# Attention on Trainium2: two query chunks side by side in the product for the maximum

## The reference

```python
h = _layernorm(x, axis=-1) * (1 + ca) + sa           # x: 16 x 512 x 256, float32
q = (h @ Wq.T).reshape(b, t, 8, 64)
kv_latent = h @ Wkv_down.T                           # 64 wide
k = (kv_latent @ Wk_up.T).reshape(b, t, 8, 64)
v = (kv_latent @ Wv_up.T).reshape(b, t, 8, 64)
scores = einsum('bqhd,bkhd->bhqk', q, k) * 64 ** -0.5
attn = softmax(scores, axis=-1)
out = einsum('bhqk,bkhd->bqhd', attn, v).reshape(b, t, 512)
x = x + ga * (out @ Wo.T)
```

## Time and profile before

| | |
|---|---|
| median of 3 runs | 1625.9 us (1625.34 to 1626.49) |
| the profiled execution | 1625.48 us, span of its instructions 1623.7 us |
| mean granted TensorE clock | 0.883 of 2.4 GHz |
| TensorE busy | 1327.1 us, 82% |
| VectorE busy | 1145.3 us, 71% |
| ScalarE busy | 740.7 us, 46% |
| GpSimd busy | 556.0 us, 34% |

### The profile page before, as it was taken

The page is one execution under the profiler, slowest core; times in us unless marked ns, Lnnn a source line. Parts: engine busy times, 40 slices in busy tenths (PEclk is TensorE's granted clock), DMA queues, the critical chain, the costliest instruction groups (busy, mean ns, idle before and its releaser), DMA issues. The chain is left out here.

```text
span 1623.7 us, 24084 instructions
## 1 busy us (share of the span) xinstructions
PE 1327.1 (82%) x5919; PEld 937.7 (58%) x5920; DVE 1145.3 (71%) x2512; ACT 740.7 (46%) x1442; POOL 556.0 (34%) x928
## 2 busy tenths in 40 slices
PE   6499999999999999999999999999511595979200
PEld 3266666666666666666666666666411595868200
DVE  2368877778777787777877778777367744656387
ACT  1366656556565565655656556564200003333052
POOL 1101423234232342323423234223310356667247
PEclk7599999999999999999999999999855556989655
DMA  4000011010110101101011010110120103232464
GB/s 108 14 14 27 1 53 49 4 52 0 53 48 4 53 0 52 47 6 52 0 53 50 3 40 1 40 40 1 44 54 0 52 0 82 36 85 33 116 220 142
DMA packets 68360, 70.29 MB, mean 43 GB/s; under 512 B 13568, under 2 KB 64176, under 8 KB 68160
## 3 DMA queue, kind: packets, MB, share of 16 engines
q1 hardware_dynamic: 44272, 44.82, 9.2%
q10 hardware_dynamic: 18960, 18.88, 3.5%
q0 software_dynamic: 5056, 5.85, 2.3%
HBM read 40.35 MB, written 28.92 MB: 43 GB/s over the span
## 5 line engine op out<-in xcount | busy, mean ns | idle before, releaser
L830 PE MATMUL PS<-PF,V 128*128 128x512 f32 x1024 | 523.9, 593 | 0.0
L561 ACT ACTIVATE PF<-PS 128x512 f32<-128x512 f32 x512 | 303.0, 595 | 345.0 <-PE PS L756 343.4
L733 DVE TENSOR_REDUCE NMAX<-PS 128x1 f32<-128x512 f32 x512 | 346.5, 687 | 160.7 <-PE PS L765 150.5
L755 PE MATMUL PS<-Q,K 128*128 128x512 f32 x512 | 405.8, 792 | 0.9 <-ACT PF L561 0.9
L531 POOL TENSOR_TENSOR XL<-XF,XH 128x512 fp32r<-128x512 f32 x64 | 84.2, 1316 | 445.7 <-ACT XH L636 445.7
L765 PE MATMUL PS<-K,Q 128*128 128x512 f32 x512 | 203.6, 398 | 6.0 <-DVE NMAX L733 5.9
L756 PE MATMUL PS<-Q,K 128*128 128x512 f32 x512 | 202.7, 396 | 0.0
L830 PEld LDWEIGHTS PS<-PF,V 128*128 128x128 f32 x1024 | 174.5, 189 | 36.2 <-issue 6.7
L579 ACT ACTIVATE Q<-PS 64x512 fp32r<-64x512 f32 x256 | 151.5, 592 | 67.8 <-PE PS L93 63.0
L755 PEld LDWEIGHTS PS<-Q,K 128*128 128x128 f32 x512 | 97.2, 190 | 123.5 <-issue 105.4
L756 PEld LDWEIGHTS PS<-Q,K 128*128 128x128 f32 x512 | 97.4, 190 | 121.7 <-issue 121.6
(11 more groups left out here) (286 smaller groups left out, 2534.6 us busy)
## 6 DMA issues: line engine op xcount, KB each, us to landing
X<-in_L_attn_x SPq DMA_DIRECT2D x16, 512.0 KB, 5.0
MODB<-mod_rows SPq DMA_DIRECT2D x16, 512.0 KB, 4.4
h_rows<-H ACTq DMA_DIRECT2D x16, 512.0 KB, 3.1
acc_rows<-H ACTq DMA_DIRECT2D x16, 512.0 KB, 4.1
A<-acc_rows SPq DMA_DIRECT2D x16, 512.0 KB, 8.3
out_x<-X SPq DMA_DIRECT2D x16, 512.0 KB, 2.9
W1F<-in_L_ffn_W SPq DMA_DIRECT2D x3, 1024.0 KB, 4.9
W2F<-in_L_ffn_W SPq DMA_DIRECT2D x3, 1024.0 KB, 5.8
```

The lines of the kernel that those rows point to most:

```text
L561: s_exp.done(act.activation(PF[:, u % 4, :], st_bank(u), ACT.Exp))
L733: s_mred.done(dve.tensor_reduce(NMAX[:, h % 2, c:c + 1], mx_bank(u), AX.X, ALU.max, negate=True))
L755: pe.matmul(st_bank(u), K1[:, kp, keys], Q1[:, h, :], start=True, stop=False)
L830: s_pv.done(pe.matmul(pv_bank(h), V1[:, vp, c, :], PF[:, u % 4, :], start=(c == 0), stop=(c == TC - 1)))
```

## The change

The contraction of the product for the maximum is cut to 64 rows: high part times high part. A second copy of the latent's high part, K3, stands in rows 64 to 127, so that a chunk can be multiplied on either half of the array. The units are taken in pairs in the even slots: the even unit uses rows 0 to 63 (Q1, K1), the odd one rows 64 to 127 (Q1, K3), and both are issued one behind the other. The pair waits for the reduce of unit u-1 in place of u-2. ScalarE makes K3 with one more copy for each batch, VectorE's L720 waits for that copy too, and the semaphore counts of the latent's copies move.

```diff
-                    ("K2", [P, 2, T], F32R), ("Q2", [P, H, T], F32R),
+                    ("K2", [P, 2, T], F32R), ("K3", [P, 2, T], F32R), ("Q2", [P, H, T], F32R),
...
-    s_exp, s_qhi, s_latc, s_v, s_nf = S("exp", UNITS), S("qhi", 16), S("latc", 3), S("vv", 1), S("nf", KC)
+    s_exp, s_qhi, s_latc, s_v, s_nf = S("exp", UNITS), S("qhi", 16), S("latc", 4), S("vv", 1), S("nf", KC)
...
                             s_latc.done(act.activation(K1[0:R, jp, :], bank[0:R, :], ACT.Copy))
                             s_vt.wait(act, jb - 1, 0)
                             s_latc.done(act.activation(LTF[:, :], bank, ACT.Copy))
+                            s_latc.done(act.activation(K3[R:P, jp, :], bank[R:P, :], ACT.Copy))
                             s_latc.wait(act, jb, 0)
                             s_latc.done(act.activation(K2[0:R, jp, :], K1[0:R, jp, :].bitcast(F32), ACT.Copy))
...
                         elif kind == "lat":
-                            s_latc.wait(dve, jb, 1)
+                            s_latc.wait(dve, jb, 2)
...
                     tb, u = unit(b, n + AHEAD)
-                    if exists(tb):
+                    if exists(tb) and u % 2 == 0:
+
                         h, c, kp = u // TC, u % TC, (par + (n + AHEAD) // UNITS) % 2
-                        s_mred.wait(pe, tb, u - 2)
+                        s_mred.wait(pe, tb, u - 1)
                         if c == 0:
                             s_qlo.wait(pe, tb, h)
+                            s_latc.wait(pe, tb, 3)
                             s_klo.wait(pe, tb, 0)
-                        s_mx.done(pe.matmul(mx_bank(u), Q1[:, h, c * P:(c + 1) * P], K1[:, kp, :], start=True, stop=True))
+                        s_mx.done(pe.matmul(mx_bank(u), Q1[0:R, h, c * P:(c + 1) * P], K1[0:R, kp, :], start=True, stop=True))
+                        s_mx.done(pe.matmul(mx_bank(u + 1), Q1[R:P, h, (c + 1) * P:(c + 2) * P], K3[R:P, kp, :], start=True, stop=True))
...
                         elif kind == "vt":
-                            s_latc.wait(pe, jb, 2)
+                            s_latc.wait(pe, jb, 1)
```

More of the change, by code:

```diff
@@ L329, in attention @@
     MODB = sb("MODB", [P, 4, D])
-    K1, K2 = sb("K1", [P, 2, T], F32R), m["K2"]
+    K1, K2, K3 = sb("K1", [P, 2, T], F32R), m["K2"], m["K3"]
     V1 = m["V1"]
```

## The result

The changed kernel takes 1694.7 us (median of 4 runs, 1694.2 to 1694.9) against 1625.6 before (median of 4; the three runs of the table above gave 1625.9): ratio 1.0428, 95% interval 1.041 to 1.0446. It is slower by 69 us, inside the range (1650 to 1738) and in the forecast's own range, 15 us under its point of 1710.

The account below looks back on a forecast made before the run. TensorE was taken to bound attention. Pairs at 4.3 us a batch plus waits at 1.0 made 5.3, over 16 batches +85 us on 1625.5: about 1710 us, own range 1690 to 1735, 8-in-10 range 1650 to 1738.

Parts of the forecast that it names:

- The bound: Attention, two thirds of the execution: TensorE is its bound, busy 1062.6 of 1068.0 us.
- The change of shape: TensorE at each pair: a 0.10 us drain each way and loads laid bare; pair +0.27 us, 4.3 a batch.
- B: Rival: no drain, overlap works, VectorE decides; about 1653 us, or 1605 if only two stretches bind; chance 0.12.
- C: Rival: neither drain nor overlap, only the waits are new, +3.4 us a batch, about 1680 us; chance 0.10.
- D: Rival: drains cost nothing, VectorE draws ahead so reduces are not late; 1566 us at full price; chance 0.07.
- the two rows: Set-up profile rows, 16 to 128 columns and 128 to 64 rows: each next load comes 0.10 us late.
- The second load, +0.11: Within a pair on TensorE: the upper half's load follows the lower half's, 0.11 us; if hidden, pair +0.16.
- What would show it: Signs in the profile after: late loads, spacing of product records, waits in slots 16 and 4, a 73.0 us batch.
- the one for the hidden load: Sign at a pair: the two product records start under 0.01 us apart if the second load is hidden.
- The late reduce: Pairs on TensorE wait for VectorE's reduce of u-1 instead of u-2: +1.0 us a batch above the pairs.
- A: Rival: drains, but the two products don't overlap; +0.39 us a pair, about 1734 us; chance 0.13.
- The K3 copy at nothing: ScalarE's extra copy, 0.62 us, is hidden by 2.3 us before L720; uncovered, 0.6 a batch, 9 us.

Follow-up runs that it names:

- the doubled pair: Changed kernel with both reduces in the even slot, each pair issued twice in a row: 1720.3 us, 55.6 above the same kernel with pairs issued once.
- the four corners: Pairs on full or 64 rows, odd reduce late or beside the even one: full 1676.6 and 1626.6 us, 64 rows 1694.7 and 1664.7 us.
- The run on one half: Changed kernel, but the second product of a pair also uses rows 0 to 63 (Q1, K1): 1734.7 us, ratio 1.067.
- full rows: Changed kernel's order, waits and K3 copy, but both products of a pair use all 128 rows: 1676.6 us, ratio 1.0314.

## Why the prediction was right, and where it was off

**The bound.** Right. TensorE was full, and what was laid on it in attention came out in the time: one more pitch a pair, in the doubled pair, came back as 55.6 us of the 60 that 256 pitches make. A batch takes 71.8 us, not 73.0.

**The change of shape.** Right in mechanism, place and size of its parts. The load of the first product starts 0.33 us after its predecessor, as given; the drain on the way back, which was my choice without a row, is the same 0.10 (0.43 from load to load is 0.11 load, 0.23 stream, 0.10 drain), and it holds for fp32r as for the float32 of set-up. Rivals B, C and D, which have no drain, fell with that. One of the two rows it was read from is weaker than I took it for. It was a step from 16 to 128 columns of weights, but in attention before the change the transpose of the maxima has 4 columns between neighbours of 128, and no drain shows on either side: each load starts with the product that was issued before it (L765 has its record at 853.39, L776 at 853.62).

```profile
853.39 0.08 PEld L776 LDWEIGHTS PS<-IDENT,NMAX 128*4 128x4 f32 x1
853.62 0.30 PEld L830 LDWEIGHTS PS<-PF,V 128*128 128x128 f32 x2 [0.15 <-issue]
```

What made the load of 18.43 late in set-up is open. The row on 128 and 64 rows, the change that the kernel makes, is the one that the runs bear out.

**The second load, +0.11: the term that was mis-sized.** I let the load for the upper half follow that for the lower one. They start together, within 0.01 us, and the pair costs +0.16 by the rows, 0.149 by the four corners (0.14 by their traces), not +0.27. 16 x 0.11 x 16 = 28 us too much. This was named as the lower end (+0.16), and of the signs under "What would show it" the one for the hidden load came true. The run on one half shows what the estimate described: a load 0.11 behind the first when both go to the same rows. With +0.16 a pair the prediction's own terms come to 2.56 + 0.92 + 0.46 + 0.1 - 0.1 = 3.9 us a batch, or about 1689 us, the lower end of its own range (1690). The 1694 that it gives for a hidden load doesn't come out of these terms, and that 1694.7 was measured is no support for it. The Trainium skill, TensorE: Matmul & The Clock Gate, section Measured speedup vs the span model, has tiles start about 4 ns apart, and the trace agrees for the products: 3 ns in the median of 256 pairs.

**The late reduce.** Right in mechanism, and larger than in the sum: a second term that was mis-sized. Slots 14 to 16: +1.08 predicted, +1.09 measured. Slots 0 to 4: +0.78 predicted and 0.78 measured. Slots 20 to 22 and 26 to 28: I gave 0.1 above the pairs for both together, and it is 0.73 - 0.16 = 0.57 and 0.26 - 0.16 = 0.10. That is 9 us too little. I had assumed that the dearer pairs would cover these delays, and for slots 20 to 22 that was wrong whatever a pair costs: the stretch is 0.73 longer here, 0.63 with full rows and 0.74 with both products on one half, where a pair costs 0.39. Like the chain of slots 14 to 16 it hangs on the product of its own first slot: after that come its reduce, the statistics, the low part of the queries (two L702) and the reduce of slot 21 (for the wait ahead of the pair of slot 22 the profile names L702 at most of the loads and the reduce at most of the products). Rival B's reading for it, +0.6, was nearer. Since the pairs are cheaper, slots 0 to 4 and 14 to 16 stand out by 0.46 and 0.93 above them and not by 0.24 and 0.81, 5 us more. The wait of slot 19 that vanished, -0.36 a batch or 6 us, I hadn't seen. Of the signs, TensorE waits in slot 16 for 0.9 us and not 0.8, in slot 4 for 0.4 and not 0.2, in slots 6 and 10 for nothing, and it also waits in slot 22, which I hadn't named.

So in attention the forecast is 28 us too high for the second load, 6 too high for the wait that went, and 14 too low for late reduces: 20 too high, and the traces have 65 us where it had 85. That the point is off by 15 us only is in part luck: the misses have different signs, and the 4 us behind attention, which the change doesn't explain, make the rest.

**The rivals.** A (no overlap), 1734: the kernel built like that takes 1734.7. That it fits to 1 us is luck as well: A lacked the +0.35 of slots 20 to 22 and the -0.36 of the wait that vanished, and the two cancel. C (only the wait), 1680: the kernel built like that takes 1676.6. The terms of B add up to +1.8 a batch and not to +1.7, which is 2 us. B and D need an array that changes shape for nothing; there is no such kernel. D's other half, that VectorE draws ahead because the second product is ready a slot earlier, comes true in slot 17 and is shown wrong by slot 16, where the pair waits for the late reduce of slot 15. Nothing here says that VectorE had no time: with the same work in another order (full-row pairs, reduces together, L720 a slot earlier) no weight load waits for it.

**The K3 copy at nothing.** Right, as far as the trace of the run with the copy alone shows; in the timed runs 1.7 us stay that it doesn't place.

## What to carry to other kernels

Running two 64-row products side by side does halve their stream, but the step from the full array and back costs about 0.20 us each way here (a drain of 0.09 to 0.10 and a load of 0.11 laid bare), so a lone pair of 512 columns loses 0.15 us; as an estimate from the doubled pair, four products in one visit would take 0.47 + 0.15 + 0.22 = 0.84 us against 0.94. That was not tried: it needs four banks for them, and all eight are taken. Before products are issued in pairs, look in the timeline at what else stands between the two instructions that free their buffers: a wait that moves from the reduce before last to the last one is a wait for everything that the other engine has queued between them. Moving the second reduce next to the first cost nothing on balance and was worth 30 to 50 us.

## What the runs showed of the hardware that I had not expected

Weight loads for different halves of the rows start together (3 ns apart in the median, both records 0.18 us), while loads for the same half come 0.11 apart. The array drains at each change between 128-row and 64-row work, in both directions and for fp32r: the next load starts 0.10 us after the stream's end. It doesn't drain between the two halves of a pair, nor for the 4-column transposes between loads of 128 columns, which keep all 128 rows. The record of a product that is held up by its own load starts with the load and is 0.10 longer (0.50 in place of 0.40 us), so that busy time goes up (TensorE 1369 us against 1327) while the array waits: the change looks like more work on the page, and only the distance between starts shows that it is waiting.
